# The query gate of a graph layer laid out with nodes and queries on partitions

## The chip, the cores and the metric

The kernel runs on one core of a Trainium2 chip. The metric is the time of one execution on the device, in microseconds (us). The kernel before took 1895.05 us, the median of 3 runs (1891.82 to 1898.16).

## The reference, cut to what matters

The program is a stack of graph layers and feed-forward layers on 256 tokens of 768 features. The change is in the first graph layer, `L0_gnn`, which runs a relational graph convolution and a gate, twice. The gate is:

```python
def _gate(h, q, Wg, bg, Wq, bq):
    B, L, F = q.shape
    N = h.shape[0] // B
    h3 = h.reshape(B, N, F)
    hg = jnp.einsum('bnf,gf->bng', h3, Wg[:, :F])
    qg = jnp.einsum('blf,gf->blg', q, Wg[:, F:]) + bg
    attn = jax.nn.sigmoid(hg[:, :, None, :] + qg[:, None, :, :])
    qi = jnp.einsum('bnlf,blf->bnf', attn, q)
    alpha = jax.nn.sigmoid(jnp.einsum('bnf,gf->bng', h3, Wq[:, :F]) + jnp.einsum('bnf,gf->bng', qi, Wq[:, F:]) + bq)
    hn = alpha * jnp.tanh(qi) + (1.0 - alpha) * h3
    return hn.reshape(B * N, F)
```

Here B is 8, L 64, F 768 and N 32. For each of 8 blocks, each of its 32 nodes meets each of 64 queries in 768 features: 12.6 million sums, sigmoids and products with `q` per layer, which are then summed over the 64 queries. There are two layers (`l` = 0 and 1); the queries' part `qg` is the same in both.

## The kernel before, in words

Each engine has a list of instructions of its own, written out by hand; engines meet through semaphores (`mark` gives the increment, `at` the value to wait for). Weights come through a ring of five slots, filled by SyncE (SP) in the order of `load`; a slot is loaded again once its last user has marked `unit_free`.

Features lie on partitions. A chunk of 128 features times a block (`it`, 6 x 8 = 48 of them per layer) is worked on in two steps of 1024 columns, 16 nodes by 64 queries. For each of the 96 steps:

- TensorE fills two PSUM banks with `hg + qg` (`gate_pe`). The two addends are kept as three bf16 parts each in `gate_rows`, tile `G`: 32 rows of nodes, 64 of queries and one of the bias, 97 in all. Six products (three parts, two banks) with the 0/1 matrix `gate_sel` make the sum. Beside each `it` stands one product of `alpha`'s argument (`beside`).
- ScalarE takes the sigmoid in place, in PSUM (`gate_act`, line 148).
- VectorE multiplies by the queries (`gate_dve`, line 120) from PSUM into an SBUF buffer of products, four of which take turns: two in `gate_work` and two in the slot of the weights `Wgh` (`weight_ring` in the profile).
- GpSimd folds the products of an `it`: it adds one half of the queries to the other (1024 columns), and for odd `it` once more (512 columns) (`gate_pool`, line 120).
- VectorE sums what is left over the queries (`qi_dve`, line 134) into `gate_qiT`.

TensorE fills a step once VectorE has multiplied the step three before. Ahead of the loop the sums `hg` are made for two halves of the nodes (`hidden_bank`), split into three bf16 parts by ScalarE and VectorE in turn, and moved within SBUF to `gate_rows` by SP (`NODE_ROWS`). For the queries this is done once, at the start (`query_pe`, `query_split_act`, `query_split_dve`, `query_rows_sp`). Behind the loop come the rest of `alpha`'s products (two of six chunks of outputs are left for then), `tanh`, and `hT += alpha * (tanh(qi) - hT)` on VectorE.

Line 114 of the profile is every matmul, 117 every transposing one, 120 every `tensor_tensor`, 134 every reduction, 148 and 151 ScalarE's activations and copies, 154 every DMA.

## Time and profile before

| | |
|---|---|
| runs | 1898.16, 1895.05 and 1891.82 us |
| profiled execution, span from its first to its last instruction | 1895.2 us |
| TensorE, matmuls busy | 1797.8 us (95%) |
| VectorE busy | 698.8 us (37%) |
| ScalarE busy | 443.6 us (23%) |
| GpSimd busy | 312.7 us (16%) |
| mean DMA rate | 192 GB/s |

The time that lies around the span is not listed apart; the span of the profiled execution is used as its time. The page cuts the span into 40 slices of 47.4 us. Counted from 1, VectorE is busy for nine tenths or more in slices 5, 6, 10, 11 and 12 alone, and nearly all of GpSimd's work lies in slices 3 to 13: these are the two gates.

### The profile page before, as it was taken

Reading aid. Unit: us, or ns where it says so; the run is one execution under the profiler, and the core shown is the slowest. Engines: PE = TensorE matmul, PEld = TensorE weight load, DVE = VectorE, ACT = ScalarE, POOL = GpSimd, SP = SyncE. Lnnn points to the kernel's source line nnn. Section 1 sums busy time; section 2 is a strip of 40 time slices with the busy share of each in tenths; the row PEclk is TensorE's granted clock in tenths of the full one; section 3 lists DMA queues with packets and bytes.
Section 4 is the critical chain, followed back from the end, with each engine's and each line's share of the span. In section 5 each row is a group of like instructions: output and inputs, shape, how many; then the busy total and the mean of one; then the engine's idle time right before and its main releaser. Section 6 shows DMA issues by size and latency. Waiting matters only on the chain.

```text
span 1895.2 us, 25780 instructions
## 1 busy us (share of the span) xinstructions
PE 1797.8 (95%) x11408; PEld 1073.3 (57%) x11408; DVE 698.8 (37%) x1265; ACT 443.6 (23%) x810; POOL 312.7 (16%) x181
## 2 busy tenths in 40 slices
PE   7999999999999999989999998887999999999999
PEld 4675445674446655668664433333575655766566
DVE  4315998019996221172321000001413232234220
ACT  0114664016662111061310000000511010131110
POOL 0013996009991000000000000000002000000000
PEclk9999999999998999999989999999999999999999
DMA  9314002402003887521449999999643245213650
GB/s 370 116 26 150 1 1 83 167 19 107 0 1 152 310 331 307 229 108 50 174 190 381 418 428 428 429 427 428 258 188 129 111 175 225 110 41 125 252 226 18
DMA packets 35275, 364.38 MB, mean 192 GB/s; under 512 B 7593, under 2 KB 10945, under 8 KB 13426
## 3 DMA queue, kind: packets, MB, share of 16 engines
q1 hardware_dynamic: 30960, 358.39, 47.3%
q10 hardware_dynamic: 4194, 4.23, 0.7%
q8 instruction: 94, 1.54, 0.3%
q14 instruction: 27, 0.22, 0.0%
HBM read 357.01 MB, written 0.79 MB: 189 GB/s over the span
## 4 chain that ended last, share of the span: by engine, by line
PE 70%; DVE 17%; DMA 11%; ACT 1%; issue 1%; SPq 0%; POOL 0%; DVEq 0%; ACTq 0%
PE banks L114 68%; DMA weight_ring<-in_L_ffn_c_fc_dram 7%; DVE weight_ring L120 5%; DVE gate_work L120 5%; DVE gate_qiT L134 4%; PE banks L117 2%; DMA weight_ring<-in_L_ffn_c_proj_e_dram 2%; DMA weight_ring<-in_L_gnn_W_in_dram 2%; DVE stat L266 1%; DVE xn_tok L125 0%; SPq L154 0%; DMA ident<-in_c_ident_dram 0%; DVE xT L137 0%; DVE stat L268 0%; ACT banks L148 0%
## 5 line engine op out<-in xcount | busy, mean ns | idle before, releaser
L114 PE MATMUL banks<-weight_ring,xT 128*128 128x384 f32 x864 | 293.5, 492 | 2.4 <-DVE rgat_xr L137 1.5
L114 PE MATMUL banks<-gate_sel,gate_rows 97*128 97x512 bf16 x1152 | 265.0, 379 | 4.4 <-DVE gate_work L120 1.4
L114 PEld LDWEIGHTS banks<-weight_ring,xT 128*128 128x128 f32 x864 | 162.6, 191 | 110.2 <-issue 10.1
L148 ACT ACTIVATE banks<-banks 128x1024 f32<-128x1024 f32 x192 | 193.3, 1008 | 100.2 <-PE banks L114 100.2
L114 PEld LDWEIGHTS banks<-gate_sel,gate_rows 97*128 97x128 bf16 x1152 | 108.2, 97 | 145.7 <-DVE gate_work L120 15.9
L114 PE MATMUL banks<-xT,weight_ring 128*128 128x256 f32 x792 | 182.2, 380 | 3.2 <-ACT x_tok L151 3.2
L120 POOL TENSOR_TENSOR gate_work<-gate_work 128x1024 f32<-128x1024 f32 (+1 forms) x72 | 143.9, 1998 | 184.1 <-DVE gate_work L120 182.3
L114 PEld LDWEIGHTS banks<-xT,weight_ring 128*128 128x128 f32 x792 | 149.7, 190 | 30.9 <-issue 4.8
L114 PE MATMUL banks<-weight_ring,r_xd 128*32 128x384 f32 (+1 forms) x2304 | 142.7, 406 | 1.0 <-DVE r_xd L124 0.6
L114 PE MATMUL banks<-weight_ring,moe_xdT 128*64 128x384 f32 x720 | 122.0, 489 | 21.4 <-DMA weight_ring<-in_L_ffn_c_fc_dram 20.4
L120 POOL TENSOR_TENSOR weight_ring<-weight_ring 128x1024 f32<-128x1024 f32 (+1 forms) x68 | 136.5, 2008 | 7.3 <-DVE weight_ring L120 5.6
L120 DVE TENSOR_TENSOR gate_work<-banks,gate_qT 128x1024 f32<-128x1024 f32 x96 | 114.7, 1218 | 1.9 <-ACT banks L148 1.8
L120 DVE TENSOR_TENSOR weight_ring<-banks,gate_qT 128x1024 f32<-128x1024 f32 x96 | 114.8, 1218 | 1.0 <-ACT banks L148 1.0
L114 PEld LDWEIGHTS banks<-weight_ring,r_xd 128*32 128x32 f32 x2304 | 76.7, 110 | 64.2 <-issue 54.5
L137 DVE COPY y_tok<-banks 128x384 f32<-128x384 f32 x32 | 17.8, 558 | 249.6 <-PE banks L117 249.6
L114 PEld LDWEIGHTS banks<-weight_ring,moe_xdT 128*64 128x64 f32 x720 | 50.6, 137 | 89.2 <-issue 54.8
L114 PE MATMUL banks<-weight_ring,y_tok 128*64 128x384 f32 x504 | 85.9, 490 | 10.1 <-DMA weight_ring<-in_L_ffn_c_proj_e_dram 10.1
L120 POOL TENSOR_TENSOR stat<-stat 128x1 f32<-128x1 f32 (+1 forms) x23 | 14.2, 615 | 428.8 <-DVE stat L124 311.0
L148 ACT ACTIVATE moe_h_tok<-banks 128x384 f32<-128x384 f32 x32 | 15.7, 490 | 267.0 <-PE banks L114 267.0
L114 PE MATMUL banks<-weight_ring,r_hT 128*32 128x192 f32 (+1 forms) x1152 | 73.2, 407 | 1.0 <-ACT r_hT L151 1.0
L114 PEld LDWEIGHTS banks<-weight_ring,y_tok 128*64 128x64 f32 x504 | 34.3, 137 | 54.6 <-issue 39.6
L2961 POOL MEMSET rgat_vecT<- 128x576 f32 x1 | 0.6, 578 | 356.2 <-PE banks L114 356.2
(369 smaller groups left out, 1969.6 us busy)
## 6 DMA issues: line engine op xcount, KB each, us to landing
weight_ring<-in_L_ffn_c_fc_dram SPq DMA_DIRECT2D x30, 2304.0 KB, 23.4
weight_ring<-in_L_ffn_c_proj_e_dram SPq DMA_DIRECT2D x21, 2304.0 KB, 28.5
weight_slot_heads<-in_L_ffn_c_proj_e_dram SPq DMA_DIRECT2D x9, 2304.0 KB, 28.3
weight_ring<-in_L_ffn_w_gate_dram SPq DMA_DIRECT2D x8, 2304.0 KB, 9.1
weight_ring<-in_L_ffn_w_up_dram SPq DMA_DIRECT2D x8, 2304.0 KB, 9.3
weight_ring<-in_L_ffn_w_down_dram SPq DMA_DIRECT2D x8, 2304.0 KB, 9.0
weight_ring<-in_L_ffn_w_dram SPq DMA_DIRECT2D x16, 1152.0 KB, 8.2
weight_ring<-in_L_gnn_W_dram SPq DMA_DIRECT2D x7, 2304.0 KB, 14.3
```

What stands on the lines that cost most here:

```text
L114: return self.e.matmul(out, lhsT, rhs, start=start, stop=stop)
L117: return self.e.transpose(out, src, self.ident[0:n, 0:n])
L120: return self.e.tensor_tensor(out, a, b, op)
L134: return self.e.tensor_reduce(out, a, AX.X, op)
L137: return self.e.tensor_copy(out, a)
L148: return self.e.activation(out, a, f, **kw)
L266: t = v.e.bn_stats(half_stats[:, c, h, :], src[:, 2 * c + h, :])
L2961: g.e.memset(rvecT[:], 0.0).then_inc(*mark("cleared", "rgat_vec"))
```

## The change

Nodes and queries go to partitions, features to columns. A step is now 8 nodes by 16 queries on the 128 partitions, times 1024 columns: four sets of 8 nodes by a third of the features (`TILE` = 256). A group `G` is one third `j` of the features and one block `b` (24 groups per layer), and has four steps `t` of 16 queries each. So there are again 96 steps per layer.

- `gate_rows` (tile `E`) holds 96 rows: 48 of queries (16 queries by three parts) and 48 of nodes (16 nodes by three parts). One product with the 0/1 matrix `selT` adds all parts at once: two products for a step (`fill_pe`) in place of six.
- The parts are first written to DRAM (`query_parts`, `node_parts`) and fetched by thirds of the features: four DMAs a group for 16 of the 24 groups inside the loop, the first eight groups ahead of it.
- ScalarE writes the sigmoid to SBUF (`products`, eight buffers in two ring slots, of which one is taken from the ring for this).
- VectorE multiplies in place in SBUF by the queries, which come laid out from DRAM, 512 KB per group, in three buffers (`gate_queries`). There is no reduction on VectorE.
- GpSimd adds the first two steps' products of each group but the last: 23 adds of 1024 columns per layer.
- TensorE sums over the queries: for each of three sets of products four products with the 0/1 matrix `selL` (32 columns) to four bands of partitions (`query_sum_pe`). The result is copied out once for each third, turned back to features on partitions (`turn_qi_pe`) and copied again.
- 60 of the 72 products of `alpha` stand inside the loop, 12 behind it.
- The bias is added to the queries' part by VectorE before its split, where it had a row of its own.
- Loads move: `W_rel2`'s second matrix and the first `w_up` are issued inside the loops, and `c_selrow` behind the second gate.

```diff
-                    for i in range(3):
-                        for k in range(2):
-                            col = (2 * q + k) * 512
-                            t = pe.mm(PS[:, step_bank(l, step) + k, :], G[0:GR + 1, i, b, f * P:(f + 1) * P],
-                                      selg[:, col:col + 512], i == 0, i == 2)
-                    t.then_inc(*mark("summed", (l, step)))
-                beside(it)
+        def fill_pe(pe, l, n):
+            G, t = divmod(n, NQL)
+            j, b = divmod(G, QB)
+            if n >= 2:
+                pe.wait_ge(*at("attended", (l, n - 2)))
+            rows = E[0:2 * PROWS, 2 * (NQL * b + t):2 * (NQL * b + t) + 2, :].rearrange("p a n -> p (a n)")
+            for s in range(2):
+                m = pe.mm(PS[:, fill_bank(n) + s, :], selT[0:2 * PROWS, s, :], rows, True, True)
+            m.then_inc(*mark("summed", (l, n)))
+
+        def query_sum_pe(pe, l, G, t):
+            j, b = divmod(G, QB)
+            c, w = b // 4, products(l, NQL * G + t)
+            for g in range(4):
+                col = (g % 2 * 2 + g // 2) * TILE
+                m = pe.mm(PS[THIRD * g:THIRD * (g + 1), QI_BANK, c * TILE:(c + 1) * TILE], selL[:, b % 4, :],
+                          w[:, col:col + TILE], b == 0 and t == 0, b == QB - 1 and t == NQL - 1)
+            return m
...
+            for n in range(STEPS):
+                G, t = divmod(n, NQL)
+                j, b = divmod(G, QB)
+                if t == 0:
+                    pe.wait_ge(*at(f"gate_rows_{b % 2}", (l, G, "nodes")))
+                fill_pe(pe, l, n)
+                if t == 0:
+                    for i in range((5 * G + 1) // 2, (5 * G + 6) // 2):
+                        beside(i)
...
+                elif t == 2 and G:
...
+                    pe.wait_ge(*at("folded", (l, G - 1)))
+                    pe.wait_ge(*at("weighed", (l, NQL * G - 1)))
+                    for u in (0, 2, 3):
+                        m = query_sum_pe(pe, l, G - 1, u)
+                    m.then_inc(*mark("qi_ps", (l, G - 1)))
...
-                a.act(PS[:, bank:bank + 2, :], PS[:, bank:bank + 2, :], ACT.Sigmoid).then_inc(*mark("attended", (l, step)))
+                if n >= 2 * NQL:
+                    a.wait_ge(*at("qi_ps", (l, G - 2)))
+                a.wait_ge(*at("summed", (l, n)))
+                a.act(products(l, n).rearrange("p (a n) -> p a n", a=2), PS[:, bank:bank + 2, :], ACT.Sigmoid
+                      ).then_inc(*mark("attended", (l, n)))
...
-                    v.tt(w4, s4, q4, ALU.mult).then_inc(*mark("weighed", (l, step)))
-                    if q == 0 and it >= 2:
-                        qi_dve(v, l, it - 2)
+            for n in range(STEPS):
+                G, t = divmod(n, NQL)
+                w4 = products(l, n).rearrange("p (a n) -> p a n", a=4)
+                q4 = bc(qrep[:, G % RBUF, t * TILE:(t + 1) * TILE].unsqueeze(1), [P, 4, TILE])
+                if t == 0:
+                    v.wait_ge(*at(f"queries_{G % RBUF}", (l, G)))
+                v.wait_ge(*at("attended", (l, n)))
+                v.tt(w4, w4, q4, ALU.mult).then_inc(*mark("weighed", (l, n)))
...
         def gate_pool(g, l):
-            for it in range(QB * DC - 1):
...
-                t = g.tt(w[:, :, 0:n], w[:, :, 0:n], w[:, :, n:2 * n], ALU.add)
-                if it % 2:
...
+            for G in range(GROUPS - 1):
+                w = [products(l, NQL * G + t) for t in range(2)]
+                g.wait_ge(*at("weighed", (l, NQL * G + 1)))
+                g.tt(w[0], w[0], w[1], ALU.add).then_inc(*mark("folded", (l, G)))
...
+        def node_parts_sp(q, l, c):
+            q.wait_ge(*at("split_lo", (l, c, 1)))
+            key = f"gate_rows_{c % 2}", (l, "node parts", c)
+            q.dma(dram["node_parts"][l, P * c:P * (c + 1)], n_parts[:, :, c, :]).then_inc(*mark(*key, 16))
+            q.wait_ge(*at(*key))
...
+        def gate_loop_sp(q, l, early):
+            for G in range(GROUPS):
+                if G + RBUF < GROUPS:
+                    queries_sp(q, l, G + RBUF)
+                if G + QB < GROUPS:
+                    q.wait_ge(*at("summed", (l, NQL * G + NQL - 1)))
+                    q.wait_ge(*at(f"gate_rows_{G % 2}", (l, G + QB - 2, "nodes")))
+                    query_rows_sp(q, l, G + QB)
+                    node_rows_sp(q, l, G + QB)
...
+                if G == 2 * QB:
+                    load(q, *early)
```

## Rows read from the trace of the kernel before

**Rows 1.** The page's chain that ended last, by line.
```profile
PE banks L114 68%; DMA weight_ring<-in_L_ffn_c_fc_dram 7%; DVE weight_ring L120 5%; DVE gate_work L120 5%; DVE gate_qiT L134 4%; PE banks L117 2%; DMA weight_ring<-in_L_ffn_c_proj_e_dram 2%; DMA weight_ring<-in_L_gnn_W_in_dram 2%; DVE stat L266 1%; DVE xn_tok L125 0%; SPq L154 0%; DMA ident<-in_c_ident_dram 0%; DVE xT L137 0%; DVE stat L268 0%; ACT banks L148 0%
```

**Rows 2.** Busy us by stretch: PE, PEld, DVE, ACT, POOL; granted clock, DMA share, GB/s.
```profile
200.00:250.00 50.00, 49.85 (x226) 24.20 (x225) 50.00 (x49) 32.97 (x35) 47.60 (x25) 1.00 0.00 1
```

**Rows 3.** Groups by form: count, busy us, mean ns, then idle time before them.
```profile
L120 DVE TENSOR_TENSOR gate_work<-banks,gate_qT 128x1024 f32<-128x1024 f32 x96 | 114.7, 1218 | 1.9 <-ACT banks L148 1.8
...
L134 DVE TENSOR_REDUCE gate_qiT<-gate_work 128x32 f32<-128x1024 f32 x24 | 29.1, 1211 | 0.0
...
L134 DVE TENSOR_REDUCE gate_qiT<-gate_work 128x32 f32<-128x512 f32 x24 | 16.3, 678 | 0.0
...
L120 POOL TENSOR_TENSOR gate_work<-gate_work 128x1024 f32<-128x1024 f32 x48 | 113.0, 2355 | 182.3 <-DVE gate_work L120 182.3
...
L148 ACT ACTIVATE banks<-banks 128x1024 f32<-128x1024 f32 x192 | 193.3, 1008 | 100.2 <-PE banks L114 100.2
```

**Rows 4.** VectorE's timeline: first and last multiplies of loops 0 and 1.
```profile
167.01 2.36 DVE L120 TENSOR_TENSOR gate_work<-banks,gate_qT 128x1024 f32<-128x1024 f32 x2 [0.35 <-ACT banks L148]
...
315.58 1.21 DVE L120 TENSOR_TENSOR weight_ring<-banks,gate_qT 128x1024 f32<-128x1024 f32 x1
...
423.60 3.49 DVE L120 TENSOR_TENSOR gate_work<-banks,gate_qT 128x1024 f32<-128x1024 f32 x3 [0.35 <-ACT banks L148]
...
571.59 1.22 DVE L120 TENSOR_TENSOR weight_ring<-banks,gate_qT 128x1024 f32<-128x1024 f32 x1
```

**Rows 5.** Groups of matmuls: the gate's filling ones, full width, 32 columns.
```profile
L114 PE MATMUL banks<-weight_ring,xT 128*128 128x384 f32 x864 | 293.5, 492 | 2.4 <-DVE rgat_xr L137 1.5
L114 PE MATMUL banks<-gate_sel,gate_rows 97*128 97x512 bf16 x1152 | 265.0, 379 | 4.4 <-DVE gate_work L120 1.4
...
L114 PE MATMUL banks<-weight_ring,r_xd 128*32 128x384 f32 x1152 | 97.4, 486 | 1.0 <-DVE r_xd L124 0.6 <-DVE r_xd L137 0.4
```

**Rows 6.** Timelines of GpSimd, then VectorE, 1434 to 1445 us.
```profile
1434.29 2.36 POOL L120 TENSOR_TENSOR small<-small,sw_bias 8x1152 f32<-8x1152 f32 x1
...
1437.93 3.76 POOL L120 TENSOR_TENSOR small<-small,sw_bias_part 8x1152 f32<-8x1152 f32 x1
1441.75 1.75 POOL L137 CAST sw_bias_part<-small 8x1152 bf16<-8x1152 f32 x1
...
1437.10 2.37 DVE L131 SCALAR_TENSOR_TENSOR rgat_E<-rgat_E 128x1536 f32<-128x1536 f32 x1 [5.17 <-ACT rgat_E L148]
1439.50 3.01 DVE L1738 CUSTOM_DVE_ANT_0 rgat_E<-rgat_E,rgat_mask 128x768 f32<-128x768 f32 x1
...
1442.43 1.88 DVE L1738 CUSTOM_DVE_ANT_0 rgat_E<-rgat_E,rgat_mask 128x768 f32<-128x768 f32 x1
```

**Rows 7.** Tiles' instructions: ns min/median/max, first and last start.
```profile
L1738 DVE CUSTOM_DVE_ANT_0 rgat_E<-rgat_E,rgat_mask x10: 948/950/3006, 1347.7 to 1442.4; 128x768 f32<-128x768 f32 x10
...
L120 DVE TENSOR_TENSOR moe_S<-iota_slot,moe_r x1: 1225/1225/1225, 975.3 to 975.3; 128x1024 f32<-128x1024 f32 x1
L120 DVE TENSOR_TENSOR moe_S<-moe_S,moe_r x1: 1226/1226/1226, 976.6 to 976.6; 128x1024 f32<-128x1024 f32 x1
```

**Rows 8.** TensorE's timeline behind loop 1.
```profile
575.30 7.07 PE L114 MATMUL banks<-gate_qiT,weight_ring 128*128 128x256 f32 x32
```

**Rows 9.** VectorE's last split in layer 0; DMAs (KB each, us to landing); best GB/s.
```profile
157.92 1.03 DVE L120 TENSOR_TENSOR gate_qiT<-gate_work,xn_tok 128x384 bf16<-128x384 f32 x2 [0.21 <-ACT xn_tok L151]
...
out_dram<-x_tok SPq DMA_DIRECT2D x2, 384.0 KB, 2.7
...
gate_rows<-xn_tok SPq DMA_DIRECT2D x32, 48.0 KB, 1.9
...
GB/s 370 116 26 150 1 1 83 167 19 107 0 1 152 310 331 307 229 108 50 174 190 381 418 428 428 429 427 428 258 188 129 111 175 225 110 41 125 252 226 18
```

**Rows 10.** TensorE's timeline at the start: the queries' part, eight blocks.
```profile
117.21 31.12 PE L114 MATMUL banks<-weight_ring,gate_qT 128*128 128x384 f32 x96
```

**Rows 11.** Busy us by stretch, as in rows 2, of a later stage.
```profile
1230.00:1240.00 10.00, 7.48 (x46) 3.23 (x48) 0.55 (x1) 0.00 (x0) 0.00 (x0) 1.00 1.02 435
```

More of the change, by code:

```diff
@@ L693, in rgcn_sp, with query_parts_sp @@
-        def rgcn_sp(q, l):
-            for r in range(NREL):
+        def query_parts_sp(q, c):
+            q.wait_ge(*at("split_lo", 2 * c + 1))
+            key = f"gate_rows_{c % 2}", (0, "query parts", c)
+            q.dma(dram["query_parts"][P * c:P * (c + 1)], q_parts[:, :, c, :]).then_inc(*mark(*key, 16))
+            q.wait_ge(*at(*key))
[3 more added lines that the diff above has]
+            q.dma(dram["node_parts"][l, P * c:P * (c + 1)], n_parts[:, :, c, :]).then_inc(*mark(*key, 16))
+            q.wait_ge(*at(*key))
@@ L695, in rgcn_sp, with queries_sp @@
+        def queries_sp(q, l, G):
+            if G >= RBUF:
+                q.wait_ge(*at("weighed", (l, NQL * (G - RBUF) + NQL - 1)))
+            elif l == 0:
+                q.wait_ge(*at("unit_free", "Wgq"))
+            else:
+                q.wait_ge(*at("agg", (1, DC // 2 - 1)))
+            q.dma(qrep[:, G % RBUF, :], dram["L0_gnn_query_rep"][G]).then_inc(*mark(f"queries_{G % RBUF}", (l, G), 16))
+        def rgcn_sp(q, l, first=0):
+            for r in range(first, NREL):
                 load(q, ("rel", l, r), dram[f"L0_gnn_W_rel{l + 1}"][r])
@@ L766, in build @@
[L766 to L777 removed]
+                for b in range(QB):
+                    if b % 2 == 0:
+                        query_parts_sp(q, b // 2)
+                    query_rows_sp(q, 0, b)
@@ new lines, in query_sum_pe, with turn_qi_pe @@
+        def query_sum_pe(pe, l, G, t):
+            j, b = divmod(G, QB)
+            c, w = b // 4, products(l, NQL * G + t)
[4 more added lines that the diff above has]
+            return m
+        def turn_qi_pe(pe, f, bank, first):
+            for c in range(TC):
+                col = first + c * P
+                t = pe.mm(PS[:, bank, col:col + P].rearrange("p (b g n) -> p b g n", b=4, g=4), qi_sb[:, c, f * P:(f + 1) * P],
+                          turn_sel, col == 0, c == 1 and (first > 0 or bank != QI_BANK))
+            return t
@@ L981, in L0_gnn_act @@
             gate_act(a, 1)
+            a.dma(selrow, dram["c_selrow"]).then_inc(*mark("consts", "first", 16))
         def L0_gnn_pool(g):
[L984 removed]
             norm_pool(g, "L0_gnn")
[L986 to L994 removed]
             for l in range(2):
@@ L3447, in _constants @@
     part = t.reshape(TC, P).T
-    sel = np.zeros((96, QN, QL), np.float32)
-    for n in range(QN):
-        sel[n, n, :] = 1.0
-        sel[QN + np.arange(QL), n, np.arange(QL)] = 1.0
+    node, query = np.divmod(np.arange(P), 16)
+    row = np.arange(48) // 3
+    sel = np.zeros((P, 2, P), np.float32)
+    for s in range(2):
+        sel[0:48, s, :] = row[:, None] == query
+        sel[48:96, s, :] = row[:, None] == 8 * s + node
+    sel_sum = (np.arange(THIRD) == (8 * np.arange(4) + node[:, None])[:, :, None]).astype(np.float32)
     selrow = np.zeros((HEADS, HEADS, P), np.float32)
```

336 lines of the change are left out of this document (174 added, 162 removed).

## The prediction

> **What bounds the kernel now.** I began with the page. TensorE's matmul line holds 68% of the chain of waits, and VectorE lines of the gate another 14% (`weight_ring`, `gate_work`, `gate_qiT`) [rows 1]. A share over the whole span says nothing of one stage, so I read the gate's two loops by themselves. A window inside loop 0 shows VectorE busy for 50.00 of 50 us, GpSimd for 47.60, ScalarE for 32.97, TensorE for 49.85, and a DMA share of 0.00 [rows 2]. The groups say what VectorE does there: per layer 96 multiplies of 1218 ns, one of whose inputs is in PSUM, and 48 reductions, 24 of 1211 ns and nearly as many of 678 ns; GpSimd folds in 2355 ns; a sigmoid takes 1008 ns [rows 3]. From the first multiply to the end of the last one the loops last 149.8 us (167.01 to 316.79) and 149.2 us (423.60 to 572.81); three multiplies in a row take 3.49 us, so one starts 1.135 us after another [rows 4]. The loops are bound by VectorE, with TensorE close behind. GpSimd's folds run beside the multiplies and cost them nothing: both kinds keep their duration.
>
> **The change, part by part.**
> *TensorE.* A record of the filling matmul costs 265.0/1152 = 0.23 us. Today a step has six, afterwards two, so 8 x 0.23 = 1.84 us for a group of four steps. An f32 product has two records; one of 256 columns costs 0.44 us (7.07 us for the 16 products of [rows 8]), and a group has 2.5 of them beside it, 1.11 us. The sums over queries are new: four products with 32 columns of weights each go to four bands of partitions. Nearest is the expert stage's product in just that form: 97.4 us for 1152 records of 384 columns, 0.68 us for a set of four (8 records), where as many full-width records take 8 x 0.34 = 2.7 us [rows 5]. Scaled to 256 columns that is 0.45 us per set, 1.35 us for three sets. Sum: 4.3 us of TensorE per group.
> *ScalarE.* It writes its 96 sigmoids to SBUF instead of PSUM. Four by 1008 ns are 4.0 us per group, with a copy now and then. No cost as long as the group takes longer.
> *VectorE.* All 48 reductions go. The 96 multiplies stay, but both inputs are now in SBUF. Alone that form costs the same: 1225 and 1226 ns for 1024 columns [rows 7]. So VectorE's own work for a group is 4 x 1.135 = 4.54 us, and had it nothing else to wait for, a loop would take 24 x 4.54 = 109 us instead of 149.5.
> *GpSimd.* 47 iterations of folding (70 operations) become 23 adds of 1024 columns, 2355 ns each by the fold of the same size [rows 3]; by a slope from smaller adds it could be some 10% less.
> *The two together.* Here lies the price. In the loops of before no VectorE instruction with two SBUF inputs meets a GpSimd add. At one place of the trace such instructions do meet [rows 6]. GpSimd's add of 8x1152 takes 2.36 us alone. The next one of the same size starts at 1437.93, while VectorE works on `rgat_E` with two SBUF inputs until 1439.47; it takes 3.76 us and ends at 1441.69, 2.22 us after VectorE let go. VectorE's next instruction, issued at 1439.50, takes 3.01 us in place of its usual 0.95 [rows 7] and ends at 1442.51, 0.82 us after GpSimd's end. Then a GpSimd cast that has waited since 1441.75 goes first, though VectorE's next one is already issued at 1442.43, and that takes 1.88 us. So they take turns, nothing runs in parallel but 0.13 us at each hand-over, and the one that waits is served at the next boundary.
> Applied to a group: GpSimd asks after the second multiply, during the third. It gets its turn when the third ends and takes 2.355 - 0.14 = 2.22 us; the fourth ends 1.22 - 0.13 = 1.09 us later; the next three take 3 x 1.135 = 3.40 us. A group takes 6.7 us. A loop is 23 x 6.7 + 4.6 (the last group has no fold) = 158.7 us, 9.2 us more than before. TensorE's 4.3 us and ScalarE's 4 us hide beneath it. The unknown is bounded by 4.54 us per group (no contention at all, -40 us per loop) and, on the other side, by VectorE and GpSimd in turn with 0.3 us more at each hand-over (7.3 us per group, +23 us per loop). I take 6.7, since the rows nearest in kind show the turns.
> The Trainium skill ("SBUF — State Buffer", "Who interferes with whom") states this for the very instruction: a `tensor_tensor` with both inputs in SBUF contends with GpSimd's reads, while one with a single SBUF input doesn't. The trace agrees for a `scalar_tensor_tensor` and a custom operation only [rows 6]; by the page the sum would be the one above, by the trace read narrowly it would be the first rival's.
> *Head of a loop.* The parts of the nodes now go out to DRAM and come back. The output's store lands after 2.7 us and a fetch of rows in 1.9 us; each fetch of a group is two DMAs [rows 9]. In layer 0 the last split ends at 158.95; the write lands at about 161.7, the rows at 164.3. Ahead of it on SP's queue stand three fetches of query rows, 512 KB each, at the 429 GB/s that the page shows at best [rows 9] 3.7 us, which may push this to 167. The first sigmoid could not run before about 165.9 anyway (the first multiply, which follows it, starts at 167.01 [rows 4]), for ScalarE is busy with the second half's splits; so up to 2 us are lost. In layer 1 these fetches were issued long before: 0. Inside the loop a group issues five DMAs, about 3 us of SP, for rows eight groups (queries: three groups) ahead of use, on queues that were idle [rows 2]. Nothing.
> *Tail of a loop.* Before, TensorE ends its products 9.5 us after the last multiply (572.81 to 582.37) since 28 products had been left over [rows 8]. After, the chain is: last sums 0.75, copy by ScalarE 0.65 (half of a 1008 ns sigmoid's columns, plus the hand-over), turning two chunks 0.6, copy 0.5, then 12 products of 0.44: 5.3, sum 7.9 us. That gives back 1.6 us per layer.
> *Start.* Eight adds of the bias on VectorE (0.5 us each by two of that size in 1.03 us [rows 9]) lengthen the chain of each split from four links to five, about 3 us. TensorE delivers the eight blocks in 31.12 us, one every 3.9 us [rows 10], so they are hidden; without that cover they would cost 8 x 0.5 = 4 us. GpSimd's bias parts and the 21 small DMAs go from places that nobody waited for. Of the weights, `W_rel2`'s third and the first `w_down` start some 7 us later, each over 20 us before its use; `c_selrow` is sent behind layer 1's gate, ahead of some 3 us of TensorE's residual work. Nothing.
> **Sum:** 2 x 9.2 - 2 x 1.6 + 2 = +17 us on the profiled span of 1895.2 us, which lies beside the median of 1895.05: 1912 us.
>
> **Rivals.**
> *No contention* (17%). If the turns belong to the instructions of [rows 6] and not to a plain multiply, a group takes 4.54 us, and TensorE's 4.3 us just fit: -40.5 per loop, -1.6 tail, +2: -82 us, 1813 us; were a group 4.8 for want of slack, 1825. For it: in the loops of before folds and multiplies ignore each other. Against it: the multiply there had only one SBUF input. It decides at a group below 6.2 us, where the loop gets shorter than 149.5.
> *GpSimd starves* (8%). VectorE's multiplies have no wait between them; if GpSimd gets no turn until VectorE stops, VectorE stops only when the fourth sigmoid of the next group is missing, because TensorE's sums wait for the fold. Then come fold 2.36, sums 1.35, fill 0.7 and sigmoid 1.0, but two folds share such a stop: (2 x 4.54 + 5.4)/2 = 7.25 us per group, +24.5 us per loop, about 1943 us. Against it stands the cast of [rows 6], served ahead of an instruction already issued. The Trainium skill says on the same page that issue order decides who blocks; by that GpSimd, which asks first, would not starve.
> *TensorE's clock falls* (5%). TensorE would be busy 4.3 of 6.7 us. At half the clock its group is 8.6 us and it becomes the bound: +57 us per loop, about 2010 us. Against it: a 10 us window with TensorE busy for 7.48 shows a granted clock of 1.00 [rows 11].
>
> **How the numbers follow.** The forecast has 70%: 1912 us, on its own 1898 to 1940 (fold 2.12 instead of 2.355 us at the low end, which gives 1901, and heads without loss; 0.3 us more at every hand-over at the high end). It alone leaves out 3 in 10, so the range reaches to the first rival: 1808 to 1940. A measurement tells about 0.3% (5.7 us) from no change. Slower by more than that: 60% from the forecast, 8% and 5% from the last two rivals, 73%. Same: 8%, the forecast's low end. Faster: the 17% and 2% of the forecast.
>
> **What would show it.** Right: VectorE's multiplies fall into two kinds, three of some 1.22 us and one above 3 us per group; GpSimd's adds last about 3.3 us, with their wait; one group every 6.7 us; TensorE busy for about two thirds of the loop. Wrong: multiplies all at 1.22 us and a loop of 110 to 120 us; or GpSimd's adds in pairs, with VectorE idle; or a granted clock below 1 in the loops; or a first fill more than 3 us after the hidden products.

## Result and profile after the change

The changed kernel takes 1922.44 us (median of 4 runs, 1920.13 to 1924.54), the kernel before it, run beside it, 1896.36 us (median of 4). The ratio is 1.0128, with a 95% interval of 1.0107 to 1.0149. So the change costs 26 us, where +17 was forecast. The profiled executions are 1918.0 and 1895.2 us long, +22.8. That difference by stage, from the timelines:

| stage | before, us | after, us | difference |
|---|---|---|---|
| start of the program to node products of layer 0 | 148.17 | 146.69 | -1.5 |
| from there to the first multiply | 18.84 | 21.60 | +2.8 |
| loop 0, first multiply to end of the last | 149.8 | 162.1 | +12.3 |
| tail 0, to the next product with `W_rel2` | 10.37 | 8.83 | -1.5 |
| from there to the first multiply of layer 1 | 96.44 | 96.46 | 0.0 |
| loop 1 | 149.2 | 160.0 | +10.8 |
| tail 1, to the residual product of `x_tok` | 9.40 | 7.86 | -1.5 |
| the rest | 1313.0 | 1314.5 | +1.5 |

The first stage and the last need care: over the profiles of this study, whose code there is the same as after or nearly so, the first lies between 146.4 and 149.2 us and the last between 1308 and 1328. So the head, the loops and the tails carry the result. (One of the four runs of the kernel `e8_queries_between`, below, was disturbed: it took 2989.01 us at a mean granted clock of 0.555, and both the time given for that kernel and its ratio leave it out.)

The page's chain that ended last, by line. The multiplies' line (`weight_ring`, L120) now has 10% by itself; before, the gate's VectorE lines had 14%, 4% of it reductions [rows 1].

```profile
PE banks L114 67%; DVE weight_ring L120 10%; DMA weight_ring<-in_L_ffn_c_fc_dram 7%; PE banks L117 2%; DMA weight_ring<-in_L_gnn_W_in_dram 2%; DMA weight_ring<-in_L_ffn_c_proj_e_dram 1%; ACT weight_ring L148 1%; DVE stat L266 1%; DMA gate_queries<-in_L_gnn_query_rep_dram 1%; DVE xn_tok L125 0%; DMA node_parts<-gate_node_parts 0%; DMA ident<-in_c_ident_dram 0%; DVE xT L137 0%; DVE stat L268 0%; DVE rgat_xr L137 0%
```

Busy time by stretch inside loop 0 (PE, PEld, DVE, ACT, POOL; granted clock, DMA share, GB/s), to be read against [rows 2]:

```profile
200.00:250.00 50.00, 37.49 (x275) 19.51 (x273) 48.73 (x30) 31.10 (x35) 25.58 (x8) 0.93 0.54 137
200.00:210.00 10.00, 7.68 (x45) 3.67 (x43) 9.25 (x6) 5.22 (x7) 5.98 (x2) 0.83 0.50 128
```

VectorE is busy for 48.73 of 50 us, nearly as before, but with 30 instructions instead of 49. Its busy time is not all work: the time for which an instruction is held up by GpSimd counts as busy too. TensorE fell from 49.85 to 37.49 and GpSimd from 47.60 to 25.58, so both have slack now. The DMA engines, idle before, have a share of 0.54.

The page's costliest groups, to be read against [rows 3, 5]:

```profile
L120 DVE TENSOR_TENSOR weight_ring<-weight_ring,gate_queries 128x1024 f32<-128x1024 f32 x192 | 308.2, 1675 | 17.4 <-ACT weight_ring L148 16.2
...
L148 ACT ACTIVATE weight_ring<-banks 128x1024 f32<-128x1024 f32 x192 | 185.5, 1026 | 134.5 <-PE banks L114 134.4
L120 POOL TENSOR_TENSOR weight_ring<-weight_ring 128x1024 f32<-128x1024 f32 x46 | 150.3, 3266 | 429.2 <-DVE weight_ring L120 429.2
...
L114 PE MATMUL banks<-weight_ring,selrow 128*32 128x256 f32 x1168 | 81.5, 413 | 79.3 <-DVE weight_ring L120 79.1
...
L114 PE MATMUL banks<-gate_rows,selrow 96*128 96x512 bf16 x384 | 112.5, 406 | 12.0 <-ACT weight_ring L148 6.8
```

A multiply of 1024 columns, 1218 ns before, now takes 1675 ns on average, and GpSimd's add of 1024 columns 3266 ns instead of 2355. The work of neither has changed; the multiply now reads its first input from SBUF. The average hides two kinds, as this row of the multiply's tile shows (least, median and greatest ns, first and last start):

```profile
L120 DVE TENSOR_TENSOR weight_ring<-weight_ring,gate_queries x192: 1209/1212/3374, 168.3 to 594.5; 128x1024 f32<-128x1024 f32 x192
```

GpSimd's timeline gives the beat of the loop. Each add starts 6.70 us after the one before it, and every one of the 22 intervals of layer 0 is 6.69 to 6.71 us.

```profile
199.45 3.26 POOL L120 TENSOR_TENSOR weight_ring<-weight_ring 128x1024 f32<-128x1024 f32 x1 [3.43 <-DVE weight_ring L120]
206.14 3.27 POOL L120 TENSOR_TENSOR weight_ring<-weight_ring 128x1024 f32<-128x1024 f32 x1 [3.43 <-DVE weight_ring L120]
...
320.03 3.27 POOL L120 TENSOR_TENSOR weight_ring<-weight_ring 128x1024 f32<-128x1024 f32 x1 [3.43 <-DVE weight_ring L120]
```

### The profile page after: what moved, and what is told of

Its sections match the earlier page's. It is cut to its first block, busy times and chain, and to the rows that moved or that the text cites. A ratio compares the mean times of both kernels' runs of the same rounds, so it can differ in the third digit from the quotient of the medians.

```text
span 1918.0 us, 26881 instructions
## 1 busy us (share of the span) xinstructions
PE 1730.7 (90%) x11856; PEld 1043.3 (54%) x11856; DVE 708.6 (37%) x1179; ACT 438.5 (23%) x816; POOL 177.0 (9%) x81
## 4 chain that ended last, share of the span: by engine, by line
PE 69%; DVE 13%; DMA 12%; issue 4%; ACT 2%; POOL 0%; SPq 0%; DVEq 0%; ACTq 0%
PE banks L114 67%; DVE weight_ring L120 10%; DMA weight_ring<-in_L_ffn_c_fc_dram 7%; PE banks L117 2%; DMA weight_ring<-in_L_gnn_W_in_dram 2%; DMA weight_ring<-in_L_ffn_c_proj_e_dram 1%; ACT weight_ring L148 1%; DVE stat L266 1%; DMA gate_queries<-in_L_gnn_query_rep_dram 1%; DVE xn_tok L125 0%; DMA node_parts<-gate_node_parts 0%; DMA ident<-in_c_ident_dram 0%; DVE xT L137 0%; DVE stat L268 0%; DVE rgat_xr L137 0%
## 5 line engine op out<-in xcount | busy, mean ns | idle before, releaser
L120 DVE TENSOR_TENSOR weight_ring<-weight_ring,gate_queries 128x1024 f32<-128x1024 f32 x192 | 308.2, 1675 | 17.4 <-ACT weight_ring L148 16.2
L148 ACT ACTIVATE weight_ring<-banks 128x1024 f32<-128x1024 f32 x192 | 185.5, 1026 | 134.5 <-PE banks L114 134.4
L120 POOL TENSOR_TENSOR weight_ring<-weight_ring 128x1024 f32<-128x1024 f32 x46 | 150.3, 3266 | 429.2 <-DVE weight_ring L120 429.2
L114 PE MATMUL banks<-weight_ring,selrow 128*32 128x256 f32 x1168 | 81.5, 413 | 79.3 <-DVE weight_ring L120 79.1
L114 PE MATMUL banks<-gate_rows,selrow 96*128 96x512 bf16 x384 | 112.5, 406 | 12.0 <-ACT weight_ring L148 6.8
L114 PEld LDWEIGHTS banks<-weight_ring,selrow 128*32 128x32 f32 x1168 | 40.8, 114 | 116.8 <-issue 95.7
L114 PEld LDWEIGHTS banks<-gate_rows,selrow 96*128 96x128 bf16 x384 | 30.2, 101 | 77.7 <-issue 33.3
L114 PEld LDWEIGHTS banks<-weight_ring,r_hT 128*32 128x32 f32 x1152 | 36.7, 110 | 37.2 <-issue 34.0
L120 DVE TENSOR_TENSOR selrow<-banks,gate_node_parts 128x384 f32<-128x384 f32 x16 | 8.5, 555 | 129.9 <-ACT gate_node_parts L151 99.9
```

What stands on the lines that cost most here:

```text
L114: return self.e.matmul(out, lhsT, rhs, start=start, stop=stop)
L120: return self.e.tensor_tensor(out, a, b, op)
L148: return self.e.activation(out, a, f, **kw)
```

## Experiments

Two questions. Is the price the turns that VectorE and GpSimd take, or a wait for the fold, or simply the multiply's new place in SBUF? And what stands beneath it: where does the loop go when the turns are gone? In all kernels the reference's whole computation is done; three of them add work on GpSimd that nothing uses, and one repeats products on TensorE. Beside them the kernel before took 1900.17, 1899.68 and 1899.72 us in the three series. An edit is shown against the changed kernel, in experiment 5 against the kernel that it starts from. Where no number of runs is given, a time comes from one run.

### 1. No fold on GpSimd

All four sets of products are summed by TensorE, and GpSimd does nothing in the loops.

```diff
-                    pe.wait_ge(*at("folded", (l, G - 1)))
                     pe.wait_ge(*at("weighed", (l, NQL * G - 1)))
-                    for u in (0, 2, 3):
+                    for u in range(NQL):
                         m = query_sum_pe(pe, l, G - 1, u)
...
         def gate_pool(g, l):
-            for G in range(GROUPS - 1):
-                w = [products(l, NQL * G + t) for t in range(2)]
-                g.wait_ge(*at("weighed", (l, NQL * G + 1)))
-                g.tt(w[0], w[0], w[1], ALU.add).then_inc(*mark("folded", (l, G)))
+            pass
```

> The changed kernel without GpSimd's 23 adds per layer; TensorE sums all four sets of products of a group instead of three. Theory (GpSimd's add and VectorE's multiply take turns): every multiply takes 1.22 us and a group falls from 6.7 us to what TensorE needs, 8 x 0.23 + 1.11 + 4 x 0.45 = 4.75 us, so a loop of about 115 us instead of 161 and a time near 1830 us, faster than the kernel before by 65 us. Rival (multiplies out of SBUF are slow in themselves, or beside the DMAs into SBUF): single multiplies above 3 us remain, the time stays at or above 1915 us.

Measured: 1871.22 us (4 runs), ratio to the kernel before 0.986 [0.9824, 0.9895]; loops 130.8 and 132.3 us. Against the changed kernel's profile 48 us are gone; I had expected a time near 1830. The tile's row, then VectorE's timeline, then one stretch, of this kernel:

```profile
L120 DVE TENSOR_TENSOR weight_ring<-weight_ring,gate_queries x192: 1216/1219/1227, 168.7 to 535.8; 128x1024 f32<-128x1024 f32 x192
```

```profile
189.94 8.04 DVE L120 TENSOR_TENSOR weight_ring<-weight_ring,gate_queries 128x1024 f32<-128x1024 f32 x7 [4.91 <-DMA gate_queries<-in_L_gnn_query_rep_dram]
...
241.48 4.63 DVE L120 TENSOR_TENSOR weight_ring<-weight_ring,gate_queries 128x1024 f32<-128x1024 f32 x4 [0.41 <-ACT weight_ring L148]
246.51 4.63 DVE L120 TENSOR_TENSOR weight_ring<-weight_ring,gate_queries 128x1024 f32<-128x1024 f32 x4 [0.40 <-ACT weight_ring L148]
```

```profile
240.00:250.00 10.00, 9.70 (x91) 4.93 (x90) 9.19 (x9) 7.65 (x8) 0.00 (x0) 1.00 0.71 182
```

All 192 multiplies take 1216 to 1227 ns with both inputs in SBUF, so the place alone costs nothing. The loop is not as short as the 115 us that I expected, for three reasons. A group takes 5.04 us, four multiplies in 4.63 and 0.41 of waiting for a sigmoid, with TensorE busy for 9.70 of 10 us: the fourth sum has nearly filled it up. VectorE waited 4.9 us in loop 0 and 7.4 us in loop 1 for the fetch of the queries. And a few single waits for a sigmoid are longer, 1.4 to 2.4 us each, among them one soon after each change to the next third of the features.

### 2. An add that nobody waits for, whole, halved, and without reads

Kernel 1, with an add on GpSimd at the fold's old place in each group. It reads and writes other tiles (`x_tok`, the spent query parts), and nobody waits for it.

```diff
+            scratch = q_parts[:].rearrange("p i c n -> p (i c n)").bitcast(F32)
+            x_flat = x_tok[:].rearrange("p c n -> p (c n)")
             for G in range(GROUPS - 1):
-                w = [products(l, NQL * G + t) for t in range(2)]
                 g.wait_ge(*at("weighed", (l, NQL * G + 1)))
-                g.tt(w[0], w[0], w[1], ALU.add).then_inc(*mark("folded", (l, G)))
+                g.then(g.tt(scratch[:, 0:1024], x_flat[:, 0:1024], x_flat[:, 512:1536], ALU.add))
```

> The kernel without the fold, with an added GpSimd add of 1024 columns per group on data that nobody uses or waits for (23 per layer). Theory of turns: the group goes back to 6.7 us, GpSimd's adds last about 3.3 us, one multiply per group 3.3 us, time about 1915 us. Rival (the loss came from TensorE's wait for the fold): nobody waits now, so the time stays within 10 us of the kernel without the fold.

In the second kernel the add has 512 columns:

> As the kernel with the unused add, but of 512 columns (1.28 us alone). Theory of turns: the delay is the add's own length less 0.27 us of overlap, so 1.0 us per group on VectorE's 4.54: 5.55 us per group, a loop of about 133 us, some 18 to 20 us per loop above the kernel without the fold (which is held by TensorE's 4.75 us), time about 1868 us. Rival (a fixed price per meeting, whatever the length): about that of the add of 1024 columns.

In the third a memset of 1024 columns, which only writes, stands in its place:

```diff
+                g.then(g.e.memset(scratch[:, 0:1024], 0.0))
```

> As the kernel with the unused add, but GpSimd writes 1024 columns with a memset (about 1 us) and reads nothing. If only reads of SBUF meet VectorE's second input, multiplies stay at 1.22 us and the time equals that of the kernel without the fold within 5 us. If any GpSimd instruction on SBUF takes the turn, one multiply per group is about 0.8 us longer and the time some 20 to 30 us above it.

Measured (one run each): 1929.43, 1884.95 and 1867.65 us; loops of 161.2 and 161.7, 139.4 and 139.6, 131.6 and 132.1 us. For each kernel the row of GpSimd's group and the row of VectorE's tile. The whole add:

```profile
L120 POOL TENSOR_TENSOR gate_query_parts<-x_tok 128x1024 f32<-128x1024 f32 x46 | 146.9, 3194 | 434.1 <-DVE weight_ring L120 434.1
...
L120 DVE TENSOR_TENSOR weight_ring<-weight_ring,gate_queries x192: 1210/1214/3376, 171.1 to 598.1; 128x1024 f32<-128x1024 f32 x192
```

The half add:

```profile
L120 POOL TENSOR_TENSOR gate_query_parts<-x_tok 128x512 f32<-128x512 f32 x46 | 97.9, 2128 | 440.0 <-DVE weight_ring L120 440.0
...
L120 DVE TENSOR_TENSOR weight_ring<-weight_ring,gate_queries x192: 1209/1214/2291, 170.6 to 553.7; 128x1024 f32<-128x1024 f32 x192
```

The memset:

```profile
L1034 POOL MEMSET gate_query_parts<- 128x1024 f32 x46 | 43.8, 952 | 477.0 <-DVE weight_ring L120 477.0
...
L120 DVE TENSOR_TENSOR weight_ring<-weight_ring,gate_queries x192: 1214/1219/1227, 169.0 to 536.7; 128x1024 f32<-128x1024 f32 x192
```

An add on which nothing depends brings the whole price back: groups of 6.70 us, and one multiply in four that is long, 3.08 us in most groups (VectorE has then already waited 0.21 us for its sigmoid) and 3376 ns at most. So it isn't a wait for the fold. The half add's groups take 5.62 us, 1.08 less, and its longest multiply is 3376 - 2291 = 1085 ns shorter: the price follows the add's length, as I expected, and isn't fixed per meeting. That kernel's loops and time still came out longer than expected (139.4 against 133 us, 1884.95 against 1868), with 2.3 and 3.9 us of waiting for queries and further waits for sigmoids. The memset costs nothing, though 45 of the 46 lie wholly beside multiplies, so what collides is GpSimd's reading.

### 3. One input from PSUM again

The changed kernel with its fold, but the sigmoid stays in PSUM and VectorE multiplies from there.

```diff
-                pe.wait_ge(*at("attended", (l, n - 2)))
+                pe.wait_ge(*at("weighed", (l, n - 2)))
...
-                a.act(products(l, n).rearrange("p (a n) -> p a n", a=2), PS[:, bank:bank + 2, :], ACT.Sigmoid
+                a.act(PS[:, bank:bank + 2, :], PS[:, bank:bank + 2, :], ACT.Sigmoid
...
-                v.tt(w4, w4, q4, ALU.mult).then_inc(*mark("weighed", (l, n)))
+                s4 = PS[:, bank:bank + 2, :].rearrange("p a (h n) -> p (a h) n", h=2)
+                v.tt(w4, s4, q4, ALU.mult).then_inc(*mark("weighed", (l, n)))
```

> The changed kernel with the fold, but the sigmoid stays in PSUM and VectorE multiplies from PSUM into the SBUF buffer, so it has one SBUF input. TensorE may refill a pair of banks only after the multiply. Theory of turns: all multiplies 1.22 us and GpSimd's adds 2.36 us although they overlap in time. The pace is then set by the two pairs of banks: fill, sigmoid, multiply and hand-overs about 3.2 us for two steps, with TensorE's sums in between: 6.4 to 7.5 us per group, so no gain in time is expected. Rival (each add delays a multiply whatever its source): one multiply per group stays near 3.3 us.

Measured: 1896.71 us; loops 150.3 and 152.8 us. The groups of this kernel:

```profile
L120 DVE TENSOR_TENSOR weight_ring<-banks,gate_queries 128x1024 f32<-128x1024 f32 x192 | 229.0, 1221 | 77.9 <-ACT banks L148 74.6 <-DMA gate_queries<-in_L_gnn_query_rep_dram 2.8 <-issue 0.3
...
L120 POOL TENSOR_TENSOR weight_ring<-weight_ring 128x1024 f32<-128x1024 f32 x46 | 108.2, 2353 | 452.8 <-DVE weight_ring L120 452.8
```

The multiplies are back to 1221 ns and the adds to 2353 ns, side by side. The turns are gone, though the fold, its order and its waits are all there. What takes their place is 74.6 us of waiting for sigmoids: with two pairs of banks, fill, sigmoid and multiply of every second step now form a chain, and a group takes 6.07 us, less than the 6.4 to 7.5 that I had expected. So reading from PSUM ends level with the kernel before (1899.68 us beside it), and 25 us behind kernel 1.

### 4. The head: query rows behind the node parts

The changed kernel with its fold; the first three fetches of `gate_queries` go out behind the node rows instead of ahead of the node parts.

```diff
-            for G in range(RBUF):
-                queries_sp(q, l, G)
             for b in range(QB):
...
                 node_rows_sp(q, l, b)
+                if b < RBUF:
+                    queries_sp(q, l, b)
```

> The changed kernel with nothing altered but the place of the first three fetches of queries, behind the first node rows. Theory (layer 0's head is late because the parts' write queues behind 1.5 MB): the write lands about 3 us after its issue instead of 6.3 us, the first fill comes about 3 us earlier, at TensorE's end of the hidden products plus 1 us, the first multiply 1.5 to 2.5 us earlier. Rival (DRAM round trip itself takes 6 us): no change. Loops keep 6.7 us a group.

Measured: 1928.19 us; from node products to first multiply 19.6 us instead of 21.60; loops 162.9 and 164.0. SP's and TensorE's timelines of the changed kernel:

```profile
155.04 1.39 SPq L154 DMA_DIRECT2D gate_queries<-in_L_gnn_query_rep_dram  x3
157.54 0.53 SPq L154 DMA_DIRECT2D node_parts<-gate_node_parts  x1
163.84 4.40 SPq L154 DMA_DIRECT2D gate_rows<-node_parts  x8
...
166.53 0.59 PE L114 MATMUL banks<-gate_rows,selrow 96*128 96x512 bf16 x2 [4.20 <-DMA gate_rows<-node_parts]
166.97 2.43 PE L114 MATMUL banks<-xT,weight_ring 128*128 128x256 f32 x6
169.19 1.79 PE L114 MATMUL banks<-gate_rows,selrow 96*128 96x512 bf16 x4
```

Those of this kernel, and VectorE's:

```profile
159.31 0.52 SPq L154 DMA_DIRECT2D node_parts<-gate_node_parts  x1
162.60 0.79 SPq L154 DMA_DIRECT2D gate_rows<-node_parts  x2
...
165.16 0.59 PE L114 MATMUL banks<-gate_rows,selrow 96*128 96x512 bf16 x2 [1.05 <-DMA gate_rows<-node_parts]
165.59 1.46 PE L114 MATMUL banks<-xT,weight_ring 128*128 128x256 f32 x6
...
168.06 10.18 DVE L120 TENSOR_TENSOR weight_ring<-weight_ring,gate_queries 128x1024 f32<-128x1024 f32 x7 [1.10 <-DMA gate_queries<-in_L_gnn_query_rep_dram]
...
192.37 7.91 DVE L120 TENSOR_TENSOR weight_ring<-weight_ring,gate_queries 128x1024 f32<-128x1024 f32 x5 [4.13 <-DMA gate_queries<-in_L_gnn_query_rep_dram]
```

From the issue of the write to the first fetch that waits for it 6.30 us pass in the changed kernel (157.54 to 163.84), behind 1.5 MB of queries, and 3.29 us here (159.31 to 162.60). So the queue did cost the head 3 us, and TensorE now idles for 1.05 us instead of 4.20. But the time didn't fall: VectorE now waits for the queries of the fourth group (group 3 in the code), 4.13 us at 192.37 and 5.24 us in layer 1. In layer 0 of the changed kernel that fetch lands 0.66 us before its use; here VectorE needs it sooner, and it lands no sooner (43.9 us behind the start of the node products, 43.0 in the changed kernel). The head was right, the gain was lost again in the loop. Part of the time above the changed kernel's (5 of 8 us by the profiles) lies in the first stage and the last, whose spread is as large.

### 5. Where the fetch of the queries goes, without the fold

Three attempts to rid kernel 1 of its waits for queries. The first takes experiment 4's order, and sends the weights that were loaded ahead of each loop late in it:

```diff
-                if G == 2 * QB:
-                    load(q, *early)
+                if G == 2 * QB or G == 2 * QB + 2:
+                    load(q, *early[G // 2 - QB])
```

> The kernel without the fold, with two orders on SyncE's queue mended: the first three fetches of queries are sent behind the first node rows, and the weight load ahead of each loop goes to group 16 of the loop. Theory (the queue carries rows, queries and weights together, and the loop without the fold needs its data faster): the two waits of VectorE for queries (4.9 and 7.4 us) and the lags after them (about 4 us) go, the head of layer 0 loses 2 us less; loops of 24 x 5.04 = 121 us; 1871 - 18 = about 1853 us. Rival (DMA throughput of the row fetches binds anyway, weights or not): waits for queries appear elsewhere and the time stays above 1865 us.

The second also puts the fetches for groups 3 and 4 between the node rows of the second half:

```diff
+                if b == 4:
+                    queries_sp(q, l, 3)
+                if b == 6:
+                    queries_sp(q, l, 4)
...
-                if G + RBUF < GROUPS:
+                if 2 <= G < GROUPS - RBUF:
                     queries_sp(q, l, G + RBUF)
```

> The kernel without the fold and with the late weight loads, and the fetches of queries for groups 3 and 4 sent between the node rows instead of behind them all. Theory (the waits of 4.9 us for queries at group 3 come from SyncE holding them back until the second half's node rows are issued, not from bandwidth): these waits fall below 1 us, the loops to 122 to 125 us, the time by some 10 us against the version without this change, about 1856 us. Rival (bandwidth): the waits remain, now on rows or later queries.

The third is the second, with TensorE's sums divided: three sets a step earlier, the last one at the old place.

```diff
+                elif t == 1 and G and b != 1:
+                    pe.wait_ge(*at("weighed", (l, NQL * G - 2)))
+                    for u in range(NQL - 1):
+                        query_sum_pe(pe, l, G - 1, u)
...
-                    for u in range(NQL):
+                    for u in range(NQL) if b == 1 else (NQL - 1,):
```

> The kernel of the next entry, and TensorE's sums of a group cut in two: three sets behind the second step's fill, one behind the third's. The last set alone then stands between VectorE's fourth multiply and the next fill. If the 0.41 us that VectorE waits per group come from that order, a group takes 4.85 us (what TensorE needs) instead of 5.04: loops of about 118 us, some 8 us in all below the next entry, about 1850 us. If TensorE's own sum binds already, no change.

| kernel | us (runs) | ratio to before | loops, us |
|---|---|---|---|
| 1 (no fold) | 1871.22 (4) | 0.986 [0.9824, 0.9895] | 130.8, 132.3 |
| late weights | 1866.86 (5) | 0.9826 [0.9802, 0.9849] | 129.7, 128.6 |
| and queries between | 1856.35 (3) | 0.9772 [0.9736, 0.9809] | 127.1, 128.5 |
| and sums in two | 1863.93 (6) | 0.9822 [0.9798, 0.9846] | 128.1, 127.7 |

VectorE's longest wait of loop 0, with late weights, then with queries between (kernel 1's is shown in experiment 1):

```profile
187.80 8.04 DVE L120 TENSOR_TENSOR weight_ring<-weight_ring,gate_queries 128x1024 f32<-128x1024 f32 x7 [4.94 <-DMA gate_queries<-in_L_gnn_query_rep_dram]
```

```profile
196.22 8.04 DVE L120 TENSOR_TENSOR weight_ring<-weight_ring,gate_queries 128x1024 f32<-128x1024 f32 x7 [3.49 <-DMA gate_queries<-in_L_gnn_query_rep_dram]
```

SP's list around the fetch for the fourth group (group 3 in the code), in kernel 1 and with late weights:

```profile
178.62 0.44 SPq L154 DMA_DIRECT2D weight_ring<-in_L_gnn_W_rel_dram  x1
179.11 0.43 SPq L154 DMA_DIRECT2D gate_queries<-in_L_gnn_query_rep_dram  x1
```

```profile
183.14 0.45 SPq L154 DMA_DIRECT2D gate_queries<-in_L_gnn_query_rep_dram  x1
```

I had put the wait down to the 2.3 MB of weights on the queue and expected it to go. In loop 0 it stayed (4.94 us), in loop 1 it fell from 7.35 to 4.87, and the time missed the 1853 us that I had expected. The weights do cost something all the same: issued right behind them, the fetch took 10.8 us to its multiply (179.11 to 189.94), without them 4.7 us (183.14 to 187.80). Counted from the start of the node products (147.02 and 149.10) it came 4.2 us earlier. But VectorE wanted it 4.3 us earlier too, since the shorter head and an earlier second sigmoid had brought the loop forward. What was left was that it went out late. Its buffer had been free since the first group's last multiply ended, about 10 us before; the second half's parts and rows stood ahead of it on SP's list.

With the queries let in between the node rows, the fetches for the fourth and fifth group landed before their use (at 176.11 and 184.78, used at 182.58 and 187.62). The wait came two groups later and 1.45 us shorter, at a fetch that was again held back: issued at 190.03, its buffer free since 182.7, behind the rows of two groups. So the reason that I had given for these waits was right, but they moved on, where I had expected less than 1 us; loops of 127.1 and 128.5 missed the 122 to 125 us expected. That the time met the expected 1856 us is luck: against the kernel with late weights it fell by 10.5 us, of which the loops gave 2.7.

The third kernel missed too: its groups alternate instead of getting shorter, since the sums now hold up the fill of another step. The waits in its timeline:

```profile
245.50 4.63 DVE L120 TENSOR_TENSOR weight_ring<-weight_ring,gate_queries 128x1024 f32<-128x1024 f32 x4 [0.74 <-ACT weight_ring L148]
250.56 4.75 DVE L120 TENSOR_TENSOR weight_ring<-weight_ring,gate_queries 128x1024 f32<-128x1024 f32 x4 [0.43 <-ACT weight_ring L148]
```

Starts lie 5.06 and 5.50 us apart, against 5.04 in kernel 1. Its two loops together are as long as those with queries between (255.8 and 255.5 us), since VectorE waits less for queries, so the 7.6 us between the two times don't come from the loops; by the profiles they lie in the last stage. The version with queries between beats both the kernel before and the changed one. It is 2.3% faster than before; against the changed kernel, by the two ratios to before (0.9772/1.0128), it is 3.5% faster.

### 6. TensorE kept busy

The changed kernel with its fold, in which TensorE does the fills of every second step three times over (the same values into the same banks), so that it idles less.

```diff
-            for s in range(2):
+            for s in (0, 1, 0, 1, 0, 1) if t % 2 else range(2):
```

> The changed kernel with its fold, but every second step's two fills are made three times (the same result, 8 records or 1.8 us of TensorE more per group of 6.7). If the groups that came later than 6.7 us did so because TensorE's clock had fallen, the granted clock stays at 1.00 in the loops and these take 159 to 160 us instead of 162 and 160, with no loss elsewhere. If TensorE's length decides instead, the loops get longer, 24 x 1.8 = 43 us at most each.

Measured: 1932.38 us; loops 162.9 and 161.4 us. The same stretch as of the changed kernel above, where TensorE was busy for 7.68 us at a granted clock of 0.83:

```profile
200.00:210.00 10.00, 9.05 (x76) 4.65 (x77) 9.26 (x8) 5.44 (x7) 4.19 (x2) 1.00 0.58 161
```

The clock is back at 1.00 (2.4 GHz), and groups take 6.70 us as before. So the lower clock, where it came, did not set the length of a group. Nor do short waits of VectorE: here it waits 0.74 us for a sigmoid in most groups, between the third multiply and the fourth, while GpSimd has its turn anyway. The loops did not shrink to the 159 to 160 us that I expected if the clock cost something. That doesn't settle what the clock costs at a loop's start, since the threefold fill stood ahead of the second sigmoid there and made VectorE wait 2.98 us for it.

## Why the prediction was right, and where its sizes were off

The forecast's mechanism was the right one, the direction too, and 1922.44 us lies in the forecast's own range. By its steps:

- *The two together.* Right, and this is the whole result. 6.7 us per group was predicted, 6.70 measured; one multiply in four is held up, 36 of these 46 for more than 3 us in all (the others had waited for a sigmoid first), and three take about 1.2 us (median 1212, greatest 3374 ns); GpSimd's adds of 3266 ns with their wait. Experiments 1 to 3 show cause: take the add away, put a memset in its place, which doesn't read, or move one input of the multiply to PSUM, and the multiply is at 1.22 us again; put an add beside it that nobody waits for, and the group is at 6.70. The row from another stage on which I had built it held for a plain multiply. The rule that I had cited from the Trainium skill ("SBUF — State Buffer", "Who interferes with whom") says the same of two inputs in SBUF against GpSimd's reads, and on that page an instruction of GpSimd that only writes is excepted; the memset of experiment 2 agrees (952 ns each, multiplies at most 1227).
- *No contention.* Refuted for this kernel. Its price was probably too good as well: with no turns at all in kernel 1 a group takes 5.04 us, and the loops 130.8 and 132.3 instead of 109 to 115. I had let TensorE's 4.3 us "just fit". Kernel 1 has a fourth sum, 4.75 us by the same rows, so it isn't quite the rival's kernel; but its waits for queries would probably have met the rival too.
- *GpSimd starves.* Refuted. The adds come singly, every 6.70 us, and each ends 2.2 us behind the end of the multiply during which it was issued.
- *TensorE's clock falls.* In part. I had named a granted clock below 1 in the loops as a sign against me, and it is there: 0.83 in eight of the 10 us stretches of the two loops and 0.93 over 200 to 250 us, so part of each such stretch was at 1.2 GHz. TensorE had been idle for a quarter of those 50 us, where it was busy for 49.85 before [rows 2]. It never became the bound of a group: the beat was 6.70 us in the stretches at 0.83 and in those at 1.00 alike, and experiment 6 shows the same. The reason is where the delay falls. In the stretches at a lower clock a sigmoid came up to 1.40 us late, but between the third multiply and the fourth, while GpSimd had its turn (at 181.63 the fourth multiply starts 1.24 us late and takes 2.06 us instead of 3.37). It cost time only at the ends of loop 0, as the next point shows.
- *Length of a loop.* This is the term that was too small: 158.7 predicted, 162.1 and 160.0 measured. The groups are exact, so the rest is at the ends, and GpSimd's adds locate it. In layer 0 the first add starts 4.35 us after the first multiply, where two multiplies in a row and the hand-over would make it 2.5, as it is in layer 1: the second sigmoid was late by 1.83 us. The last add starts at 320.03 and the last multiply ends at 330.40, which is 10.4 us where layer 1 has 8.9: the last sigmoid was late by 1.38. In layer 1 one interval is 7.95 instead of 6.70, with 1.17 us of waiting for queries. 1.9 + 1.5 and 1.25 us account for all of 3.4 and 1.3. The late second sigmoid follows a fill that started 2.66 us after the first, behind six records of `alpha`'s products that took 2.43 us; TensorE had idled for 4.20 us before the first fill, and the granted clock was 0.72 over 166 to 169 us. In experiment 4, where it had idled for 1.05 us, the clock was 1.00 over 165 to 168 us, the same six took 1.46 and the second fill came 1.72 us after the first. So about 0.9 of the 1.83 us went with the clock. The late last sigmoid goes with it too: TensorE's sums ahead of it took 2.79 us where the clock was 0.83, and 1.50 in layer 1 at 1.00, where nothing was late, and the last group has no add to hide it:

```profile
324.53 2.79 PE L114 MATMUL banks<-weight_ring,selrow 128*32 128x256 f32 x24 [2.02 <-DVE weight_ring L120]
...
591.29 1.50 PE L114 MATMUL banks<-weight_ring,selrow 128*32 128x256 f32 x24 [2.02 <-DVE weight_ring L120]
```

- *Head of a loop.* "Up to 2 us" became 2.8. The mechanism was as described, the queries' fetches ahead of the node parts, but it took longer than priced: 6.30 us from the issue of the write to the first fetch behind it. Of these 3.29 are the write's (experiment 4), where I had taken 2.7 from a store of 384 KB for one of 576, and 3.0 came from the queries ahead of it. Layer 1's head cost nothing, as said (96.44 and 96.46).
- *Tail.* 1.6 us to be gained per layer, 1.5 measured (the terms of the forecast add up to 7.8, not 7.9), to be seen in TensorE's timeline behind loop 0:

```profile
331.80 1.16 PE L114 MATMUL banks<-ident,selrow 128*128 128x128 f32 x8 [0.70 <-ACT selrow L151]
332.97 5.45 PE L114 MATMUL banks<-gate_qiT,weight_ring 128*128 128x256 f32 x24
339.23 13.14 PE L114 MATMUL banks<-weight_ring,xT 128*128 128x384 f32 x40 [0.82 <-DVE xT L120]
```

- *In the loop, DMA: "nothing".* Wrong in kind, though it cost only 1.2 us here, since a group of 6.70 us hides most of it. With groups of 5.04 us it costs 4.9 and 7.4 us (kernel 1). I had counted SP's time to issue the fetches, but neither their order on its list, where the fourth group's stands behind the second half's rows and the weights (experiment 5), nor the load on the DMA engines: a share of 0.54 at 137 GB/s.
- *Start.* Hidden, as predicted, as far as it can be told (-1.5 us, within the spread).

In sum: forecast +17, profile +22.8. The ends of loop 0 and loop 1's wait for queries add 4.7, the head 0.8; the rest is spread. The medians lie 26 us apart, 3 us more than the profiles; the changed kernel's profile is of the fastest of its four runs.

What stays open: how much of the remaining waits for queries in the kernels without a fold comes from the load on the DMA engines. That the weights and SP's order delay these fetches is read from the traces; no run sent each fetch as soon as its buffer was free, and none changed the size of the rows' pieces. What made up the other 0.9 us of the late second sigmoid in layer 0 wasn't separated either.

## What to carry to other kernels

Before an input of VectorE is moved from PSUM to SBUF, look at what GpSimd does at that time: an instruction with two inputs in SBUF and a GpSimd instruction that reads there run one after the other, and here some 90 us of removed reductions (2 x (29.1 + 16.3) [rows 3]) bought nothing, because 46 adds by 2.22 us, 102 us, came on top of the multiplies. A GpSimd operation that seems free in a profile is free only beside the instructions that it runs beside there; when VectorE's next instruction reads both inputs from SBUF, it has a price. And when a bound is removed, price the next one from its own rows (here TensorE at 9.70 of 10 us, and fetches that had landed 0.7 us before their use) before promising what the engine could do alone.

## What the runs showed of the hardware

- The hand-over is quick: an add of 2.36 us that is issued during a multiply ends 2.2 us behind that multiply's end, though VectorE's next multiply is ready. Four multiplies and one add take 6.70 us with an add of 1024 columns and 5.62 us with 512. A sigmoid that comes up to 1.40 us late costs nothing if it is the one for the multiply that would be held up anyway.
- The clock was granted at 0.83 in a stretch in which TensorE was busy for 7.68 of 10 us (200 to 210 us of the changed kernel), and at 1.00 in one with 6.49 (240 to 250 us).
- The write of the node parts (576 KB) to DRAM and the fetch that waits for it were issued 3.29 us apart without the queries ahead of them, and 6.30 us behind three fetches of 512 KB. In kernel 1 a fetch of 512 KB took 10.8 us right behind one of 2.3 MB; the median of such fetches in the changed kernel is 4.0 us.
